# One attention layer and a routed feed-forward block on one core: GpSimd's running sum of probabilities cut into instructions of at most 512 columns, with the next step's diagonal selected halfway through

## What is computed

```python
scores = jnp.einsum('bhki,bhqi->bhkq', k, q) / math.sqrt(HEAD)     # keys x queries
mask = jnp.arange(n)[:, None] <= jnp.arange(n)[None, :]
scores = jnp.where(mask, scores, jnp.float32(-10000.0))
attn = jax.nn.softmax(scores, axis=2)
combined = jnp.einsum('bhkq,bhkl->bhql', attn, v)
out = combined.transpose(0, 2, 1, 3).reshape(b, n, HIDDEN)
return out @ W_out + b_out
```

## Time and profile before

| | us |
|---|---|
| median of three runs | 2622.0 |
| lowest, highest run | 2616.1, 2622.58 |
| the profiled execution, its device time | 2616.99 |
| the span in its profile, first to last instruction | 2615.3 |
| mean granted TensorE clock, share of full speed | 0.985 |

### The profile page before, as it was taken

One profiled execution on the slowest core, in us unless ns is written; L12 is line 12 of the kernel. 1 busy time (PEld: TensorE's weight loads), 2 busy tenths in 40 slices (PEclk: granted clock), 3 DMA queues, 4 the chain that ended last, 5 costly groups with the idle time before them and its releaser, 6 DMA issues.

```text
span 2615.3 us, 40182 instructions
## 1 busy us (share of the span) xinstructions
PE 2527.0 (97%) x13920; PEld 1805.3 (69%) x13920; DVE 1742.1 (67%) x4231; ACT 1235.6 (47%) x2354; POOL 1530.9 (59%) x1232
## 2 busy tenths in 40 slices
PE   7999999999999999999999999998899999999998
PEld 5665666666666666666666666664588888888886
DVE  6667678777777876877787787778465435544533
ACT  2565655666565665655665665665631111111110
POOL 1667787777787777778777787776231213122211
PEclk8999999999999999999999999998999999999999
DMA  7556667676566766657676576764431101001010
GB/s 146 89 102 138 126 139 164 134 149 156 106 149 126 164 146 129 158 122 142 128 176 126 122 174 118 144 128 130 154 105 33 41 25 36 22 26 40 17 33 17
DMA packets 167260, 286.43 MB, mean 110 GB/s; under 512 B 23121, under 2 KB 58001, under 8 KB 165906
## 3 DMA queue, kind: packets, MB, share of 16 engines
q1 hardware_dynamic: 159890, 267.01, 47.5%
q0 software_dynamic: 7168, 16.85, 2.0%
HBM read 116.97 MB, written 65.11 MB: 70 GB/s over the span
## 4 chain that ended last, share of the span: by engine, by line
PE 82%; DVE 6%; POOL 4%; ACT 4%; issue 2%; DMA 2%; SPq 0%; ACTq 0%; POOLq 0%; DVEq 0%
PE PS L1451 13%; PE PS L1430 13%; PE PS L1380 10%; PE PS L1396 10%; PE PS L1300 9%; PE PS L1349 9%; PE PS L1314 7%; PE PS L1308 7%; POOL Pa L771 4%; PE PS L1323 2%; DVE xTl L1087 2%; DVE PS L998 1%; DVE nm L990 1%; DMA Qp<-nat 1%; ACT PS L928 1%
## 5 line engine op out<-in xcount | busy, mean ns | idle before, releaser
L771 POOL TENSOR_TENSOR Pa<-Pa,Pm 128x1024 f32<-128x1024 f32 (+2 forms) x332 | 707.6, 2147 | 167.9 <-ACT Pm L893 116.7
L1380 PE MATMUL PS<-Qp,Kp 98*128 98x512 f32 (+3 forms) x1536 | 547.4, 361 | 18.7 <-ACT P L893 6.5
L893 ACT ACTIVATE Pm<-PS 128x512 f32<-128x512 f32 (+3 forms) x856 | 396.6, 470 | 335.8 <-PE PS L1380 321.6
L1349 PE MATMUL PS<-Kp,Qp 96*128 96x512 f32 (+3 forms) x1536 | 504.2, 364 | 26.1 <-DVE nm L998 14.4
L990 DVE TENSOR_REDUCE nm<-PS 128x1 f32<-128x512 f32 x512 | 344.6, 685 | 217.7 <-PE PS L1349 217.1
L1380 PEld LDWEIGHTS PS<-Qp,Kp 98*128 98x128 f32 x1536 | 291.6, 192 | 223.3 <-ACT Pm L893 92.3
L771 POOL TENSOR_TENSOR Pa<-Pa,P 128x1024 f32<-128x1024 f32 (+2 forms) x164 | 349.8, 2149 | 78.5 <-ACT P L893 55.1
L1349 PEld LDWEIGHTS PS<-Kp,Qp 96*128 96x128 f32 x1536 | 283.1, 193 | 108.2 <-issue 33.8
L860 ACT ACTIVATE G<-PS,b1c 128x512 f32<-128x512 f32 x128 | 88.2, 689 | 539.6 <-PE PS L1430 520.6
L998 DVE CUSTOM_DVE_ANT_0 PS<-PS,maskA 128x384 f32<-128x384 f32 (+3 forms) x512 | 244.9, 506 | 134.7 <-PE PS L1349 133.1
L1451 PE MATMUL PS<-W2h,Gs 128*128 128x512 f32 x1024 | 316.6, 390 | 0.9 <-DVE W2l L1092 0.9
(11 more groups left out here) (142 smaller groups left out, 4181.1 us busy)
## 6 DMA issues: line engine op xcount, KB each, us to landing
Qp<-nat SPq DMA_DIRECT2D x192, 256.0 KB, 6.6
Kp<-nat SPq DMA_DIRECT2D x192, 256.0 KB, 6.0
o_s<-Of SPq DMA_DIRECT2D x64, 256.0 KB, 2.2
Ot<-o_s SPq DMA_DIRECT2D x64, 256.0 KB, 3.2
xb<-in_x SPq DMA_DIRECT2D x64, 256.0 KB, 3.4
h_s<-hs SPq DMA_DIRECT2D x64, 256.0 KB, 3.4
out<-xb SPq DMA_DIRECT2D x64, 256.0 KB, 3.5
x_raw<-in_xt SPq DMA_DIRECT2D x15, 1024.0 KB, 6.8
```

The lines of the kernel that those rows point to most:

```text
L771: e.tensor_tensor(to, to, tile[:, h0:h0 + many, 0:w], ALU.add).then_inc(s["padd"], many // 2)
L893: e.activation(probs(u, k)[:, h_, 0:w], PS[:, B_BANKS[j % 2], 0:w], ACT.Exp).then_inc(s["b_exp"], 1)
L1349: ins = e.matmul(to, Qp[0:96, u % 4, h_, qt * P:qt * P + P], Kp[0:96, (2 * i + k0 // 512) % 4, h_, 0:w], start=True, stop=True)
L1380: e.matmul(PS[:, B_BANKS[j % 2], 0:w], Kp[0:98, (2 * i + k // 4) % 4, h_, k % 4 * P:k % 4 * P + P], Qp[0:98, u % 4, h_, 512 - w:512], star ...
```

## The change

Four things change, all for the units that add on POOL. An add instruction covers 512 columns at most: one head where the width is 512 or 384, two heads at 256, four at 128 as before. The semaphore `padd` counts four a step instead of two, and its three readers with it. The select of step `k + 1` is moved into the addition of step `k`, in front of head 2, for all steps of the diagonal but the first one that has a select in an odd unit (step 4) and the first two of an even unit (`kept_early`). And POOL waits for the exponentials of a step in front of its add only where there is no select of that step to wait for.

```diff
+def kept_early(u, k):
+
+    return not by_products(u) and k >= 2 and diag(u, k - 1) is not None and k < ksteps(u)
...
+            def keep(u, k):
+                tile = probs(u, k)
+                e.wait_ge(*formed(u, k))
+                e.affine_select(out=tile[:, :, 0:P], in_=tile[:, :, 0:P], compare_op=ALU.is_ge, fill=0.0, base=0,
+                                pattern=[[0, HG], [1, P]], channel_multiplier=-1).then_inc(s["keep"], 1)
+
             for n in range(T.first, T.last):
                 for u, k in T.steps_formed(n):
-                    tile = probs(u, k)
-                    e.wait_ge(*formed(u, k))
                     i = diag(u, k)
-                    if i is not None:
-                        e.affine_select(out=tile[:, :, 0:P], in_=tile[:, :, 0:P], compare_op=ALU.is_ge, fill=0.0,
-                                        base=0, pattern=[[0, HG], [1, P]], channel_multiplier=-1).then_inc(s["keep"], 1)
+                    if i is not None and not kept_early(u, k):
+                        keep(u, k)
                     a = added(u, k)
                     if a is not None and not by_products(u):
                         if i is not None:
                             e.wait_ge(s["keep"], i + 1)
-                        e.wait_ge(s["padd"], 2 * a)
+                        else:
+                            e.wait_ge(*formed(u, k))
+                        e.wait_ge(s["padd"], 4 * a)
                         if k == 1:
                             e.wait_ge(s["pv"], ksteps_before(u) + 1)
                         w = width(u, k)
-                        many = 2 if w > 256 else 4
+                        many = 1 if w > 256 else 2 if w > P else HG
                         for h0 in range(0, HG, many):
+                            if h0 == 2 and kept_early(u, k + 1):
+                                keep(u, k + 1)
                             to = acc[:, u % 2, h0:h0 + many, 512 - w:512]
-                            e.tensor_tensor(to, to, tile[:, h0:h0 + many, 0:w], ALU.add).then_inc(s["padd"], many // 2)
+                            e.tensor_tensor(to, to, probs(u, k)[:, h0:h0 + many, 0:w],
+                                            ALU.add).then_inc(s["padd"], many)
```

More of the change, by code:

```diff
@@ L887, in scalar @@
                                 e.wait_ge(s["pv"], ksteps_before(u0) + k0 + 1)
-                                e.wait_ge(s["padd"], 2 * (a - 2))
+                                e.wait_ge(s["padd"], 4 * (a - 2))
                             elif k0 == ksteps(u0) - 1:
@@ L1260, in wait_ready @@
                     if not by_products(u):
-                        e.wait_ge(s["padd"], 2 * added_before(u + 1))
+                        e.wait_ge(s["padd"], 4 * added_before(u + 1))
                 elif kind == "C":
```

## The result

Five runs of the changed kernel gave a median of 2609.01 us (2608.61 to 2611.27), and five of the kernel before on the same chip 2619.0 us (2615.21 to 2622.58). The ratio is 0.9965, with a 95% interval of 0.9953 to 0.9976: faster by 9 us, between 6 and 12. The profiled execution took 2609.01 us (span 2607.3) where that of before took 2616.99 (span 2615.3), 8.0 us less. Forecast were 2610 us for the median and 2605 for the profiled execution.

The account below looks back on a forecast made before the run. PE, busy 97% of the span, was taken as the bound, so time could only come from its gaps. -13.8 - 1 + 2.2 + 0.5 = -12.1 us, and 2622 - 12 = 2610 us, range 2598 to 2628.

Parts of the forecast that it names:

- Part 1, the six units: Units 13, 21, 29, 37, 45, 53: shorter adds halve DVE's mean wait, PE gains 2.3 us a unit, 13.8 us.
- Part 2, POOL's price: Four adds of 512 columns take 5.00 us against 4.73 for two of 1024; 434 more instructions are 59 us of POOL.
- e: POOL's extra time for each added instruction: 0.135 us, taken from the two add shapes.
- Part 2, the early units: Units 1, 3 and 7: later select and last add cost PE 0.75 us each, +2.2 us.
- Part 3, the early select: Select k+1 moves forward by half an add, behind a wait for its exponentials; effect on the last product 0.
- tied units: Twenty odd units where PE's last product starts 0.14 us after the select of step 7, with no slack.
- Unit 61: Select of step 5 now precedes the layer norm's factors: counted 0 to +0.9 us, taken as +0.5.
- the last rival: With e near 0.05, all 20.8 us of PE's waits on DVE go, and 1.7 in unit 5: 2600 us; chance 0.1.
- The select holds PE: Tied and early units lose by a later select 7, which also cuts the six units' gain: 2630 us; chance 0.12.
- Costs and gain cancel: DVE's stalls shrink, but POOL ends the chain; gain per unit 1 us in place of 2.3: 2619 us; chance 0.18.
- The change does not shorten DVE's waits: DVE waits until POOL's queue is empty, so only costs stay: 2625 us; chance 0.08.
- It goes all the way: With e near 0.05, PE's 20.8 us of waits on DVE and 1.7 in unit 5 go: 2600 us; chance 0.1.

## Why the prediction was right, and where it was off

**Part 1, the six units: right in mechanism and size.** Predicted 2.3 us a unit, 13.8 in all; measured 14.9 between units 9 and 53. It was capped where the text had put the cap, at the select of step 7, and that wait stands in all six units, not only in four. PE's waits on DVE fell to 1.8 us (predicted under 5), the median `xTl` to 1.18 us (predicted near 1.3). That there was more behind the cap than its 8.7 us is what the adds of one column show.

**Part 2, POOL's price: right for an undisturbed add.** In unit 31 four adds of 512 columns, and then two, take this:

```profile
943.11 5.01 POOL L783 TENSOR_TENSOR Pa<-Pa,P 128x512 f32<-128x512 f32 x4
...
948.80 2.53 POOL L783 TENSOR_TENSOR Pa<-Pa,Pm 128x512 f32<-128x512 f32 x2
...
961.40 0.63 POOL L760 TENSOR_SCALAR_AFFINE_SELECT Pm<-Pm 128x512 f32<-128x512 f32 x1
```

2 x 1.28 - 0.04 = 2.52 was expected for two and 5.00 for four, against 4.73 for two long ones. So e = 0.135 us stands, and the 0.06 us that the prediction works out from the Trainium skill, page "GPSIMD Engine Reference", does not. POOL's busy time rose by 67.6 us where 59 were forecast. I did not split the other 9; interruptions by DVE are likely, as the mean add of 1.33 us lies above 1.28.

**Part 2, the early units: the step that failed.** The text put +2.2 us on units 1, 3 and 7 and -1 on unit 5, +1.2 us together; it was +7.7. Two things were mis-sized. First, PE's wait for the select grew by 0.81, 0.47 and 0.48 us in units 1, 3 and 7 where 0.35 was taken, and in unit 5 from 0.62 to 2.59 us. DVE's gain of 1 us there was taken back because POOL holds PE next, which the text had named and then given too little weight. It was no worse because the wait of 2.55 us for the DMA of `Qp`, 6 us behind that product before, is gone; the text had passed over the waits on DMAs in this stretch. From unit 3's last product to unit 6's it is 80.04 us where it was 79.60. Second, and larger, the price of a wait was taken as its length, and the clock behind it was put at nothing. The stretch from the last product of unit 1 to that of unit 2 grew by 2.7 us (19.19 to 21.93), and that from unit 7 to unit 8 by 2.8. Behind the wait at its start neither holds a wait of PE above 0.5 us, before or after. These two are 5.5 of the 7.7 us, and gains and losses elsewhere leave 2.2. That is one pair of executions, and some of it is chance: the second stretch came out 2.4 us shorter in the run with short adds in the first eight units alone, and the first one differed by 2.6 us between two runs with long adds there, each time with the same instructions and a wait at its start equal to 0.02 us. The window of 120 to 130 us of the kernel before, at a clock of 0.83, could have warned of it. Long adds in the first eight units removed the loss and short adds there alone brought most of it back, which settles where it comes from: by the ratios 9 us in the one and 5 in the other. How much of that is clock and how much wait is open. Over 60 to 350 us the clock is 0.94 and 0.95 in the profiles of the two kernels with short adds there and this placing of select and sum, and 0.96 to 0.98 in the four with long adds there and the same placing; but a single wait doesn't settle the clock behind it.

**Part 3, the early select: right.** It was costed at nothing, and alone it measures 0.9998. In the tied units the last product starts 0.19 us after its select (962.22 against 961.40 + 0.63) with no idle time, and the profile lists no wait there. That it is necessary was said only through its rival; without it the kernel is 1.2% slower than the kernel before, and 1.5% slower than the changed one.

**Unit 61: the wait at its upper bound, the end better than its lower one.** ACT's exponential behind the layer norm's factors is late, and PE waits for it:

```profile
1796.73 0.58 PE L1393 MATMUL PS<-Qp,Kp 98*128 98x256 f32 x1 [6.12 <-ACT P L906]
```

The wait is 0.87 us longer, as the 0.9 of the select and two more instructions in front of the factors. I had taken half of that. From unit 53 to the end the trace is nonetheless 0.8 us shorter (1031.3 to 1030.5), so other waits gave back more than this.

**The sum.** Early units +7.7 for +1.2, six units -14.9 for -13.8, the end -0.8 for +0.5: -8.0 in place of -12.1. The median came nearer (2609 for 2610) since it was taken from the 2622 of three runs, where the five here give 2619. So the forecast of the median is good in part by chance, and that of the difference is 3 us too large. The chances have a slip as well: 0.62 for a gain of over 8 us is the whole 0.52 of the forecast's range and the last rival's 0.1, and leaves nothing for that range's upper end, which the next sentence counts among "the same".

**The rivals.** *The select holds PE* did not happen, but its pattern is right, as the kernel without the early select shows at 2652.58 us. *Costs and gain cancel* had the gain per unit at 1 us and is out by the 2.5 measured. Some of its point came true elsewhere: half of the gain was cancelled, in the early units. *The change does not shorten DVE's waits* is out by `xTl`. *It goes all the way* is out for this change, and the run with adds of one column shows that it was there to be had.

## What to carry to other kernels

Where two engines take turns on a port by the instruction, cut the long instructions of the one that is not urgent, but only beside the other's urgent ones: here seven units of 64 carried the gain, and the same cut in the first eight, where the cutting engine was itself the one waited for, gave back half of it. Count a wait of PE with a possible fall of the clock behind it, and read the clock of the windows behind the existing waits first; since that fall comes and goes with the same instructions, compare such stretches over several executions. And when a deadline of a late engine is moved, look which of its next deadlines is now hit. Moving the select alone or the sum alone gave nothing that the times show, and both, with long adds in steps 1 and 2, took the ratio from 0.9927 to 0.9874.

## What the runs showed of the hardware

- The granted clock behind a wait of PE isn't fixed by the wait. Means over the next 10 us were 0.53 after 2.89 us idle (unit 1), 0.66 after 2.59 (unit 5), and 0.66 after 1.74 (units 3 and 7); 1.00 after 1.27 and 1.26 in the kernel before. With the same instructions as the changed kernel up to there, 1.72 us in unit 7 left it at 1.00 in another run; and 1.24 us in unit 1 went with 1.00 in one run and 0.66 in another. In the later units 1.46 us left it at 1.00 all six times. A fall in that place costs some 2.5 us. What decides it these runs don't show.
- An add that waits by semaphore for the add before it starts some 0.17 us after that one ends, as at 1128.34 us in unit 37. For the adds of 512 columns above this kind of idle time comes to 13.9 + 7.5 = 21.4 us in the changed kernel. It was hidden where a select stood between the two.
- Where DVE gets in between two instructions of POOL, the one behind took some 0.45 us longer in the places looked at: a select takes 0.64 us alone, and 1.09 and 1.10 in unit 37, before and after.
